# Block products in the first experts' second product and in the fourth attention layer

## The chip, the cores and the metric

One core of one Trainium2 chip runs the whole program. The metric is the device time of one execution in microseconds, the median of three runs. The shares and timelines below come from one profiled execution of the same program.

## The reference, cut to what matters

Two layers of a graph transformer on 1250 nodes with 768 channels, all in float32. Each layer adds graph attention (two attention layers each) and a kernel-feature mixer to its input, then a mixture of experts:

```
x = x + gnn0(ln(x)) + mix0(ln(x))
x = x + ffn0(ln(x))       # 2 of 4 experts, chosen once for all rows
xn = ln(x)
x = x + gnn1(xn) + mix1(xn)
x = x + ffn1(ln(x))

# ffn0, each chosen expert e, its activation gelu, silu, mish or gelu:
h = act_e(x @ w1[e] + b1[e])          # 768 -> 1536
out += gate_e * (h @ w2[e] + b2[e])   # 1536 -> 768

# gnn, each attention layer:
h = x @ W; e = leaky_relu(h@a_src [src] + h@a_dst [dst])
alpha = softmax of e over the edges of each target
out = sum over edges of alpha * h[src] + b
```

## The kernel before

The graph is turned into a dense 1250 x 1250 matrix of edge counts early on, and attention is done densely: for a group of 250 targets the weights ET1 (exp, times the counts) are made for all 1250 sources, and their product with the features HN1 gives the outputs; a column of ones behind the features gives the sum of the weights. Rows come in 10 tiles of T = 125 or in 5 pairs of 250; HALF is 384 channels. Five engines run their own instruction lists and meet in semaphores. TensorE writes into two rings of PSUM banks: five "V" banks that VectorE reads, three "A" banks that ScalarE reads. `plan()` lists the order in which names take banks; `fill` makes TensorE wait until the bank's last user is read (`v_drained` or `a_drained`), and reads are counted in the order of the list.

The experts (PE lines 799 to 805, ScalarE 1229 to 1262, VectorE 1845 to 1955) run 11 iterations u; a unit u is one expert e = u // 5 and one pair of tiles. TensorE makes the first product of unit u in six blocks of 2 x 128 hidden channels (matmuls of 128 x 250, six per 128 channels), then the second product of unit u - 1: four banks, each 12 matmuls of 384 columns. ScalarE drains each block into HB with the bias, then an exp (L1240) one block behind it (three behind in unit 1); `gelu(u)` (L1232) works on the whole unit, for unit 0 behind the third block of unit 1. VectorE computes from the exp the ratio that silu and mish need, in `clamp` (L1848) and `ratio` (L1856 to L1866, seven operations in all on 128 x 500), combines it with the Gelu (L1930), and adds the four banks of unit u - 1, times the gate, to XN (L1948). From u = 6 on it also takes statistics (`pair_output`), from u = 7 on the layer's norm and residual (`pair_residual`, which takes a slot that SP loads) and the next norm (`pair_next`). SP's list issues the DMAs in order: `residual` stores a tile, waits until it is stored and, by its `reused`, until `pair_next` has read it, loads the tile after next and then calls `mixer_load`, which loads the next mixer's weights: WQ lies over the experts' scratch memory, and `q1` (the next mixer's first product) waits for it.

The fourth attention layer's product is `gat1(3)`: five groups of 250 targets, each four banks (two tiles of targets, two halves of channels) of 10 matmuls (one per tile of sources). VectorE makes a group's weights with `larger` (L1720) and a multiply by the counts (L1772) from ScalarE's two rows of exps (`step1`, L1126 and L1131, which for group i start when group i - 2's last bank is full); `drain_group` (L1730 to L1741) divides by the sum of weights, adds to Y, takes statistics, and in tiles 5 and 7 makes the scale of a norm group with `scale`, which waits for ScalarE's square root (`deviation`, L1023); for tile 5 that stands in ScalarE's list behind `step1` of group 4.

The last experts' product and the second mixer's k and v already use block products: for a product of 2 x 2 blocks, seven products of sums of blocks in place of eight, in banks a, b and c that are read and refilled between them.

Of the kernel before, what the change touches and what calls it, by code (L numbers as in the profile page):

```python
# [47 lines left out]
SLOPE = 0.2  # L48
H0, C0 = 4, 192
# [42 lines left out]
def plan():  # L92
# [6 lines left out]
    def gat(layer):  # L99
# [17 lines left out]
        elif layer == 2:  # L117
            for g in range(5):
                V.extend((("acc", 2, g, 0), ("sum", g), ("acc", 2, g, 1), ("acc", 2, g, 2)))
        else:  # L120
            V.extend(("acc", layer, g, i) for g in range(5) for i in range(4))
# [47 lines left out]
    for u in range(11):  # L169
        if u < 10:  # L170
            A.extend(("f1", u, i) for i in range(6))
        if u > 0:
            V.extend(("f2", u - 1, i) for i in range(4))
# [31 lines left out]
def gps_kernel(nc, w, out):  # L205
# [16 lines left out]
    with ctx:  # L222
# [72 lines left out]
        CO = small(16)  # L295
        IS = small(2, 4)
# [70 lines left out]
        TURNED = [mem(C_AT + 6250, 2, 250), mem(C_AT + 6750, 2, 250), mem(F_AT + 11536, 2, 250)]  # L367
        WSUM = [ROW[3][:, i * 250:(i + 1) * 250] for i in range(2)]
# [10 lines left out]
        def hn_pair(layer, t, half):  # L379
            if layer == 0:  # L380
# [11 lines left out]
        EB = mem(C_AT, HM, 250)  # L392
        TB = mem(C_AT + 3000, HM, 250)
        SLOT_F = [mem(C_AT + 6000 + i * D, D) for i in range(2)]
# [72 lines left out]
        prow_loaded = [sem(f"target_rows_loaded{i}") for i in range(2)]  # L467
        slopes_made, larger_made = sem("slopes_made"), sem("larger_made")
# [10 lines left out]
        clamped, expd, t_made, gelu_made, act_made = (sem("hidden_clamped"), sem("hidden_exp"), sem("hidden_exp_used"),  # L479
                                                      sem("gelu_made"), sem("hidden_made"))  # L480
# [23 lines left out]
        def _(pe):  # L504
# [250 lines left out]
            def gat1(layer):  # L755
                gat_front(layer)
                pe.wait_ge(a_drained, A_AT[("h", layer, NT - 1, 1)] + 1)
                for g in range(5):
                    pe.wait_ge(et_made, 80 + (layer - 2) * 5 + g + 1)
                    for tt in range(2):  # L760
                        for p in range(2):
                            b = fill("V", ("acc", layer, g, 2 * tt + p))
                            n = HALF + p
                            for j in range(NT):
                                last = mm(b[0:T, 0:n], ET1[g % 2][0:T, j, tt * T:(tt + 1) * T],
                                          HN1[0:T, j, p * HALF:p * HALF + n], j == 0, j == NT - 1)
                            last.then_inc(v_filled, 1)
# [1876 lines left out]
```

## Time and profile before

| what | us |
|---|---|
| median of 3 runs | 2624.5 (2624.4 to 2626.75) |
| the profiled execution | 2625.9 |
| its span | 2624.1 |
| TensorE busy | 2554.6, 97% |
| VectorE busy | 1586.3, 60% |
| ScalarE busy | 769.3, 29% |

A float32 matmul shows as two records in the trace. The first experts' stage runs from 1010 to 1627 us, the fourth attention layer's product from 2267 to 2396 us.

### The profile page before, as it was taken

The numbers are of one execution on the slowest core, as the hardware profiler recorded it, in microseconds if no ns is written. First come the engines' busy times: TensorE is split into PE (matmuls) and PEld (weight loads), VectorE is DVE, ScalarE is ACT, GpSimd is POOL, SyncE is SP. The second block draws the span as 40 slices with busy tenths as digits, with TensorE's granted clock in tenths as the row PEclk, the third lists the DMA queues.
The fourth block names the chain that finished last, engine by engine and source line by source line (L and its number), as shares of the span: only waits on it lengthen the run. The fifth ranks groups of instructions, "written<-read, shape, count | busy, mean of one in ns | idle before, by whom it ended". The sixth has DMA issues, their size and how long they took to land.

```text
span 2624.1 us, 26650 instructions
## 1 busy us (share of the span) xinstructions
PE 2554.6 (97%) x10594; PEld 1815.0 (69%) x10594; DVE 1586.3 (60%) x2708; ACT 769.3 (29%) x1291; POOL 346.9 (13%) x197
## 2 busy tenths in 40 slices
PE   7999999999999997999999999999999999999999
PEld 4667667658966996777777775565755786556676
DVE  4456471789948996988888998254342561341422
ACT  1143343006733763222222221430002331332000
POOL 0888888000000000000000000000000000000000
PEclk9999999999999998999999999999999999999999
DMA  9232313543020406000120003100450100213201
GB/s 257 26 43 14 50 2 50 140 157 114 20 80 27 110 1 215 1 0 1 72 102 0 24 24 122 64 1 1 119 160 18 37 1 1 64 36 126 87 24 59
DMA packets 139168, 160.74 MB, mean 61 GB/s; under 512 B 96618, under 2 KB 108484, under 8 KB 137516
## 3 DMA queue, kind: packets, MB, share of 16 engines
q1 hardware_dynamic: 68323, 158.60, 19.5%
q0 software_dynamic: 70720, 0.43, 2.8%
q8 instruction: 84, 1.38, 0.2%
q14 instruction: 41, 0.34, 0.0%
HBM read 122.75 MB, written 35.87 MB: 60 GB/s over the span
## 4 chain that ended last, share of the span: by engine, by line
PE 52%; DVE 7%; ACT 2%; issue 1%; DMA 0%; SPq 0%; DVEq 0%; ACTq 0%
PE psum L521 51%; DVE arena L1864 2%; DVE arena L1865 1%; DVE arena L1866 1%; PE psum L532 0%; DVE arena L1857 0%; ACT arena L1126 0%; ACT arena L1131 0%; ACT arena L1015 0%; DVE arena L1519 0%; DVE arena L1930 0%; DVE arena L1361 0%; DVE arena L1863 0%; DVE arena L1856 0%; DVE arena L1889 0%
## 5 line engine op out<-in xcount | busy, mean ns | idle before, releaser
L521 PE MATMUL psum<-arena 128*125 128x384 f32 (+12 forms) x9762 | 2453.4, 413 | 33.9 <-DMA arena<-in_ffn_w 7.2
L521 PEld LDWEIGHTS psum<-arena 128*125 128x125 f32 (+3 forms) x9762 | 1719.4, 188 | 744.1 <-issue 134.7
L2279 POOL DMA_INDIRECT count_matrix<-arena x170 | 342.2, 2013 | 121.5 <-DVE arena L1458 59.6
L1864 DVE RECIPROCAL arena<-arena 128x500 f32<-128x500 f32 x60 | 196.7, 3278 | 2.1
L1613 DVE CUSTOM_DVE_ANT_0 arena<-arena 125x1250 bf16<-125x1250 bf16 (+1 forms) x100 | 139.2, 1458 | 11.7 <-DMA arena<-source_rows 7.1
L2289 POOL MEMSET arena<- 125x60 f32 x1 | 0.2, 211 | 1039.6 <-PE psum L521 1039.6
L1698 DVE TENSOR_TENSOR arena<-arena 125x1250 f32<-125x1250 f32 x80 | 116.3, 1453 | 12.9 <-ACT arena L1108 12.2
L1105 ACT ACTIVATE arena<-arena 125x1250 f32<-125x1250 f32 x80 | 106.9, 1336 | 54.5 <-PE psum L521 54.3
L1701 DVE SCALAR_TENSOR_TENSOR arena<-arena 125x1250 f32<-125x1250 f32 x80 | 116.9, 1461 | 2.8
L1015 ACT ACTIVATE arena<-psum 128x250 f32<-128x250 f32 (+1 forms) x102 | 40.6, 495 | 231.4 <-PE psum L532 230.9
L1248 ACT ACTIVATE arena<-psum,arena 128x250 f32<-128x250 f32 x120 | 49.3, 465 | 199.0 <-PE psum L521 199.0
L1058 ACT ACTIVATE arena<-arena 32x500 f32<-32x500 f32 (+1 forms) x108 | 59.1, 548 | 164.7 <-DVE arena L1492 163.9
L1108 ACT ACTIVATE arena<-arena 125x1250 f32<-125x1250 f32 x80 | 105.8, 1322 | 0.0
L1150 ACT ACTIVATE arena<-psum 125x384 f32<-125x384 f32 x80 | 38.5, 487 | 223.9 <-PE psum L521 123.8
L532 PE MATMUL psum<-arena 125*128 125x125 f32 x420 | 60.0, 290 | 24.0 <-DVE arena L1380 10.8
L1240 ACT ACTIVATE arena<-arena 128x500 f32<-128x500 f32 x60 | 37.3, 621 | 140.0 <-DVE arena L1848 139.9
L1126 ACT ACTIVATE arena<-arena 125x250 f32<-125x250 f32 x100 | 40.4, 490 | 116.4 <-PE psum L521 116.4
L532 PEld LDWEIGHTS psum<-arena 125*128 125x128 f32 x420 | 47.7, 148 | 37.7 <-issue 18.9
L1720 DVE TENSOR_TENSOR arena<-arena 125x2500 f32<-125x2500 f32 x10 | 27.6, 2764 | 72.8 <-ACT arena L1131 72.8
L1631 DVE TENSOR_SCALAR arena<-arena 125x40 f32<-125x40 f32 (+1 forms) x4 | 0.7, 178 | 106.5 <-ACT arena L1150 78.3
L1490 DVE TENSOR_SCALAR arena<-psum,arena 96x500 f32<-96x500 f32 (+1 forms) x36 | 23.3, 647 | 66.0 <-PE psum L521 65.5
L1848 DVE TENSOR_SCALAR arena<-arena 128x500 f32<-128x500 f32 x60 | 25.0, 420 | 61.1 <-ACT arena L1248 59.7
(226 smaller groups left out, 1437.2 us busy)
## 6 DMA issues: line engine op xcount, KB each, us to landing
arena<-in_ffn_w SPq DMA_DIRECT2D x3, 4608.0 KB, 14.8
residual<-arena SPq DMA_DIRECT2D x30, 336.0 KB
arena<-residual SPq DMA_DIRECT2D x30, 336.0 KB
arena<-target_rows SPq DMA_DIRECT2D x12, 610.4 KB
arena<-in_gat_w SPq DMA_DIRECT2D x3, 2304.0 KB, 10.9
arena<-residual SPq DMA_DIRECT2D x10, 672.0 KB
residual<-arena SPq DMA_DIRECT2D x10, 672.0 KB
count_matrix<-arena SPq DMA_DIRECT2D x2, 3125.0 KB, 26.5
```

The costliest lines, as they stand in the source:

```text
L521: return pe.matmul(o, lhsT, rhs, start=start, stop=stop, skip_group_check=share)
L532: last = pe.transpose(b[:, i * T:(i + 1) * T], source[0:T, t0 + i, k * 128:(k + 1) * 128], IDENT[0:T, 0:T])
L1015: act.activation(o, i, ACT.Copy).then_inc(a_drained, 1)
L1058: act.activation(o[low, cols], t[32 * i:32 * i + 32, cols], ACT.Square)
L1105: act.activation(ET4[n % 4][0:T, :], PROWS[layer][h % 2][0][0:T, :], ACT.Exp, bias=ASC[0:T, h, j:j + 1])
L1108: act.activation(E24[n % 2][0:T, :], PROWS[layer][h % 2][1][0:T, :], ACT.Exp, bias=AS2[0:T, h, j:j + 1]).then_inc(slopes_made, 1)
L1248: last = act.activation(HB[u % 2][:, m, :], b[:, j * 250:(j + 1) * 250], ACT.Identity, bias=B1C[:, e, m:m + 1])
L1613: ins = dve.tensor_tensor_reduce(SUMS[n % 2][0:T] if layer < 2 else E24[n % 2][0:T, :], NEG[0:T, t, :], ASROWS[layer][h % 2][0:T, :], 1.0, ...
L1698: dve.tensor_tensor(et, et, E24[n % 2][0:T], ALU.max).then_inc(larger_made, 1)
L1701: dve.scalar_tensor_tensor(et, et, 1.0, CT[0:T, j, :], ALU.min, ALU.mult).then_inc(et_made, 1)
L1864: now(dve.reciprocal(t_, t_))
L2279: pool.indirect_dma_start(counts[k], bass.IndirectOffsetOnAxis(ap=IDX_I[0:T, c:c + 1].bitcast(U32), axis=0), COUNT_I[0:T, c:c + 1], None, ...
```

## The change

In the experts' second product the 12 blocks of 128 hidden channels are split: the first six, as 2 x 2 blocks of three with the two tiles of rows and the two halves of channels, go through seven products of three matmuls; the last six go through four runs of six matmuls, added in the same banks. Five matmuls of 385 columns in each of seven products replace the 40 of a group in the fourth attention layer. `down0`, on TensorE:

```
+            def down0(u):
...
+                bank_d, bank_b, bank_c, bank_a = (fill("V", ("f2", u, i)) for i in "dbca")
+                n = 4 * u
...
+                product(1, bank_a, True).then_inc(parts_filled, 1)
+                pe.wait_ge(hidden_sums, u + 1)
+                pe.wait_ge(w2_sums, u // 5 + 1)
+                product(5, bank_b, True).then_inc(parts_filled, 1)
+                rest(1, 1, bank_d, True)
+                pe.wait_ge(parts_read, n + 1)
+                product(6, bank_a).then_inc(parts_filled, 1)
+                pe.wait_ge(parts_read, n + 2)
+                product(3, bank_b, False, False)
+                rest(0, 1, bank_b)
+                pe.wait_ge(parts_read, n + 3)
+                product(7, bank_a).then_inc(parts_filled, 1)
+                product(2, bank_c, True, False)
+                rest(0, 0, bank_c)
+                pe.wait_ge(parts_read, n + 4)
+                product(4, bank_a, False, False)
+                rest(1, 0, bank_a)
```

On ScalarE the exp reads HB (no clamp before it), with a scale per expert, into one of two small buffers, and a Square follows it; Gelu works in place. On VectorE:

```
+                dve.tensor_scalar(t_, EB[n % 2], BIG, 1.0, ALU.min, ALU.add).then_inc(exp_read, 1)
+                dve.wait_ge(exp_read, n + 1)
+                now(dve.reciprocal(t_, t_))
+                now(dve.tensor_scalar(t_, t_, c(NCK), c(KO), ALU.mult, ALU.add))
+                ins = dve.tensor_tensor(t_, t_, h, ALU.mult)
...
+            def weight2_sums(e):
+                dve.wait_ge(f2_loaded[e], 16)
...
+                now(dve.tensor_tensor(W2T[0], w12, w11, ALU.subtract))
+                now(dve.tensor_tensor(W2T[1], w22, W2T[0], ALU.subtract))
+                step(dve.tensor_tensor(W2T[2], w21, W2T[1], ALU.subtract))
+                now(dve.tensor_tensor(w12, w22, w12, ALU.subtract))
...
+            def sums_of_hidden(u):
...
+                now(dve.tensor_tensor(HS0, a21, a22, ALU.add))
+                step(dve.tensor_tensor(HS1, HS0, a11, ALU.subtract))
+                now(dve.tensor_tensor(a21, a11, a21, ALU.subtract))
+                step(dve.tensor_tensor(HS3[0], a12[:, 0:1], HS1[:, 0:1], ALU.subtract))
+                now(dve.tensor_tensor(HS3[1], a12[:, 1:3], HS1[:, 1:3], ALU.subtract))
```

The sums of W2 are of 1152 columns each, those of the hidden block of 375 (three), 125 and 250.

VectorE's order in an iteration of the experts (`add_part` reads a bank that is filled again, `add_bank` frees one):

```
             for u in range(11):
                 if u < 10:
+                    for i in range(4):
+                        if (u, i) == (6, 3):
+                            weight2_sums(1)
+                        ratio(u, i)
+                if u > 0:
+                    down = {x: bank(("f2", u - 1, x)) for x in "dbca"}
+                    add_part(u - 1, 1, "a", 0, 0)
+                    add_part(u - 1, 2, "b", 1, 1)
+                if u < 10:
+                    ratio(u, 4)
+                if u > 0:
...
+                    add_bank(u - 1, "d", 1, 1)
+                    add_part(u - 1, 3, "a", 0, 1)
+                if u < 10:
+                    ratio(u, 5)
+                if u > 0:
...
+                    add_bank(u - 1, "b", 0, 1)
...
+                    add_part(u - 1, 4, "a", 1, 1)
+                if u < 10:
...
                     dve.wait_ge(gelu_made, u + 1)
+                    dve.scalar_tensor_tensor(HB[u % 2], HB[u % 2], KG[:, e:e + 1], TB, ALU.mult, ALU.add).then_inc(act_made, 1)
...
+                    sums_of_hidden(u)
                 if u == 0:
                     last_bias()
+                    weight2_sums(0)
+                if u == 10:
+                    pair_residual(3)
+                if 7 <= u < 10:
                     pair_residual(u - 7)
                 if u == 10:
                     pair_next(3)
                 if u > 0:
...
+                    add_bank(u - 1, "c", 0, 0)
+                    add_bank(u - 1, "a", 1, 0)
...
+                if u < 5:
+                    add_bias(u)
                 if u >= 6:
                     pair_output(u - 6)
                 if 7 <= u < 10:
                     pair_next(u - 7)
```

The fourth attention layer, TensorE and then VectorE (`spread(g)`, whose banks b, c, a hold 385 columns; RAW keeps three raw sums in SBUF until their weight sum is whole):

```
+                    product(1, bank_a, parts_filled, True)
+                    pe.wait_ge(weight_sums_made, g + 1)
+                    product(5, bank_b, parts_filled, True)
+                    pe.wait_ge(hn_sums, 1)
+                    pe.wait_ge(parts_read, SPREAD_PARTS + 4 * g + 1)
+                    product(6, bank_a, parts_filled)
+                    pe.wait_ge(parts_read, SPREAD_PARTS + 4 * g + 2)
+                    product(3, bank_b, v_filled)
+                    pe.wait_ge(parts_read, SPREAD_PARTS + 4 * g + 3)
+                    pe.wait_ge(hn_sums, 3)
+                    product(7, bank_a, parts_filled)
+                    product(2, bank_c, v_filled, True)
+                    pe.wait_ge(parts_read, SPREAD_PARTS + 4 * g + 4)
+                    product(4, bank_a, v_filled)
...
+                    part(1)
+                    dve.tensor_copy(r00, bank_a[0:T, wide]).then_inc(parts_read, 1)
...
+                    part(2)
+                    dve.tensor_copy(r11, bank_b[0:T, wide]).then_inc(parts_read, 1)
...
+                    part(3)
+                    dve.tensor_copy(r01, bank_a[0:T, wide]).then_inc(parts_read, 1)
+                    if g < 4:
+                        larger(n, g + 1)
...
+                    dve.tensor_tensor(r01, r01, bank_b[0:T, wide], ALU.add).then_inc(v_drained, 1)
+                    if g < 4:
+                        weights(n, g + 1)
+                    part(4)
+                    dve.tensor_tensor(r11, r11, bank_a[0:T, wide], ALU.add).then_inc(parts_read, 1)
+                    if g < 4:
+                        block_sums(n, g + 1)
...
```

Behind that `spread` makes two reciprocals and adds the four halves, times them, to Y, the last two when banks c and a are full; statistics, variance and `scale` follow as before. For group 0 the sums of features (HNT, 1925 columns each) stand between the parts.

SP's list:

```
-                    load(WQ, w["mix1_wq"], m1w[0])
+                    load(WQ[:, 0:5], w["mix1_wq"][:, 0:5], m1w[0])
                 if t == 9:
-                    vf(("f2", 9, 3))
+                    vf(("f2", 9, "b"))
+                    load(WQ[:, 5:6], w["mix1_wq"][:, 5:6], m1w[0])
+                    for k, name in ((1, "mix1_bo"), (2, "mix1_bk"), (3, "mix1_bv")):
+                        row_load(k, name, m1_small)
+                    vf(("f2", 9, "a"))
                     load(WF[1], w["mix1_wk"], m1w[1])
```

The three row loads stood behind the load of the second expert's W2 before. `q1` waits for both parts of WQ.

## Rows read from the trace of the kernel before

**Rows 1.** the page: busy time of each engine and its instructions.
```profile
PE 2554.6 (97%) x10594; PEld 1815.0 (69%) x10594; DVE 1586.3 (60%) x2708; ACT 769.3 (29%) x1291; POOL 346.9 (13%) x197
```

**Rows 2.** waits of TensorE: for whom, us, times, longest.
```profile
PE psum L521 <- DVE arena L1948: 0.6, 1, 0.6
```

**Rows 3.** timeline, VectorE, units 5 and 6: start us, us, line.
```profile
1342.99 3.34 DVE L1930 SCALAR_TENSOR_TENSOR arena<-arena 128x3000 f32<-128x3000 f32 x1
...
1404.30 3.34 DVE L1930 SCALAR_TENSOR_TENSOR arena<-arena 128x3000 f32<-128x3000 f32 x1
```

**Rows 4.** timeline, ScalarE, drains of two blocks of unit 7.
```profile
1426.57 0.83 ACT L1248 ACTIVATE arena<-psum,arena 128x250 f32<-128x250 f32 x2 [2.30 <-PE psum L521]
...
1431.63 0.83 ACT L1248 ACTIVATE arena<-psum,arena 128x250 f32<-128x250 f32 x2 [3.72 <-PE psum L521]
```

**Rows 5.** windows, fourth attention product: us, busy (instructions), granted clock, DMA.
```profile
2266.00:2396.00 130.00, 129.40 (x401) 1.00 0.14 49
```

**Rows 6.** windows, TensorE, while pairs of the second mixer run.
```profile
1716.00:1780.00 64.00, 64.00 (x200) 1.00 0.00 0
```

**Rows 7.** timeline, VectorE, reciprocals of two ratio steps in turn.
```profile
1426.11 3.28 DVE L1864 RECIPROCAL arena<-arena 128x500 f32<-128x500 f32 x1
...
1433.11 3.28 DVE L1864 RECIPROCAL arena<-arena 128x500 f32<-128x500 f32 x1
```

**Rows 8.** groups of VectorE: count, busy us, mean ns, idle before.
```profile
L1864 DVE RECIPROCAL arena<-arena 128x500 f32<-128x500 f32 x60 | 196.7, 3278 | 2.1
...
L1857 DVE TENSOR_TENSOR arena<-arena 128x500 f32<-128x500 f32 x60 | 40.7, 679 | 2.1
...
L1930 DVE SCALAR_TENSOR_TENSOR arena<-arena 128x3000 f32<-128x3000 f32 x10 | 33.4, 3344 | 0.4
...
L1856 DVE TENSOR_SCALAR arena<-arena 128x500 f32<-128x500 f32 x60 | 32.1, 536 | 11.8 <-ACT arena L1240 11.3
...
L1848 DVE TENSOR_SCALAR arena<-arena 128x500 f32<-128x500 f32 x60 | 25.0, 420 | 61.1 <-ACT arena L1248 59.7
...
L1948 DVE SCALAR_TENSOR_TENSOR arena<-psum,arena 125x384 f32<-125x384 f32 x40 | 22.4, 611 | 6.4 <-PE psum L521 6.2
...
L1978 DVE TENSOR_TENSOR arena<-arena 128x375 f32<-128x375 f32 x9 | 4.9, 541 | 0.0
...
L1965 DVE TENSOR_TENSOR arena<-arena 128x1152 f32<-128x1152 f32 x2 | 2.7, 1358 | 0.1
```

**Rows 9.** timeline, ScalarE, unit 1: Gelu of unit 0, sixth block's drain.
```profile
1060.79 2.70 ACT L1232 ACTIVATE arena<-arena 128x3000 f32<-128x3000 f32 x1
...
1073.83 0.83 ACT L1248 ACTIVATE arena<-psum,arena 128x250 f32<-128x250 f32 x2 [0.52 <-PE psum L521]
```

**Rows 10.** timeline, units 9, 10: residual, bank adds, SP's DMAs, transposes.
```profile
1593.78 0.17 DVE L1881 RECIPROCAL arena<-arena 125x2 f32<-125x2 f32 x1
...
1603.00 2.19 DVE L1948 SCALAR_TENSOR_TENSOR arena<-psum,arena 125x384 f32<-125x384 f32 x4
...
1609.47 0.79 SPq L2305 DMA_DIRECT2D residual<-arena  x2
...
1613.19 0.75 SPq L2305 DMA_DIRECT2D arena<-residual  x2
...
1626.99 2.94 PE L532 MATMUL psum<-arena 125*128 125x125 f32 x24
```

**Rows 11.** timeline, attention product, start of group 3.
```profile
2344.48 4.05 ACT L1126 ACTIVATE arena<-arena 125x250 f32<-125x250 f32 x10 [17.86 <-PE psum L521]
...
2353.78 0.21 ACT L1023 ACTIVATE arena<-arena 125x4 f32<-125x4 f32 x1
```

**Rows 12.** windows, timeline: TensorE after stops of 2.85, 1.45, 5.27 us.
```profile
144.00:148.00 4.00, 2.64 (x6) 0.61 0.68 121
...
612.00:616.00 4.00, 4.00 (x26) 1.00 1.03 411
...
990.17 5.03 PE L532 MATMUL psum<-arena 125*128 125x125 f32 x24 [5.27 <-ACT arena L1034]
```

More of the change, by code:

```diff
@@ L757, in gat1 @@
                 pe.wait_ge(a_drained, A_AT[("h", layer, NT - 1, 1)] + 1)
-                for g in range(5):
[L759 to L767, printed above, removed]
+                low, high = slice(0, 5), slice(5, 10)
@@ L1231, in gelu @@
                 act.wait_ge(t_made, u + 1)
-                act.activation(EB, HB[u % 2], ACT.Gelu).then_inc(gelu_made, 1)
+                act.activation(HB[u % 2], HB[u % 2], ACT.Gelu).then_inc(gelu_made, 1)
             for u in range(10):
@@ L1236, in _ @@
                 act.wait_ge(b1_loaded, 32)
+                act.wait_ge(choice_made, 1)
                 def expo(i):
-                    act.wait_ge(clamped, 6 * u + i + 1)
-                    act.activation(EB[:, 2 * i:2 * i + 2, :], TB[:, 2 * i:2 * i + 2, :], ACT.Exp).then_inc(expd, 1)
+                    n = 6 * u + i
+                    if n >= 2:
+                        act.wait_ge(exp_read, n - 1)
+                    act.wait_ge(a_drained, A_AT[("f1", u, i)] + 1)
+                    x = EB[n % 2]
+                    act.activation(x, HB[u % 2][:, 2 * i:2 * i + 2, :], ACT.Exp, scale=SCL[:, e:e + 1]).then_inc(act_step, 1)
+                    own[0] += 1
+                    act.wait_ge(act_step, own[0])
+                    act.activation(x, x, ACT.Square, bias=MISH[:, e:e + 1]).then_inc(expd, 1)
                 lag = 3 if u == 1 else 1
@@ new lines, in block_sums @@
+                def block_sums(n, g):
+                    dve.wait_ge(et_made, n + 1)
+                    et = ET1[g % 2][0:T]
+                    a11, a12, a21, a22 = (et[:, 5 * j:5 * j + 5, i * T:(i + 1) * T] for i in range(2) for j in range(2))
+                    now(dve.tensor_tensor(ES0[0:T], a21, a22, ALU.add))
+                    step(dve.tensor_tensor(ES1[0:T], ES0[0:T], a11, ALU.subtract))
+                    now(dve.tensor_tensor(a21, a11, a21, ALU.subtract))
+                    dve.tensor_tensor(ES3[0:T], a12, ES1[0:T], ALU.subtract).then_inc(weight_sums_made, 1)
@@ L1761, in drain_turned @@
                             dve.engine_nop().then_inc(v_drained, 1)
-                drain = drain_turned if layer == 2 else drain_group
-                if layer == 2:
-                    dve.wait_ge(ct_loaded, 32)
+                if layer == 3:
+                    dve.wait_ge(a_drained, A_AT[("h", 3, 4, 1)] + 1)
+                    first = step(dve.tensor_tensor(HNT[0][0:T], hn[0][1], hn[0][0], ALU.subtract))
+                    larger(85, 0)
+                    weights(85, 0)
+                    dve.wait_ge(a_drained, A_AT[("h", 3, 9, 1)] + 1)
+                    after(first)
+                    block_sums(85, 0)
+                    feature_sum(1, hn[1][1], HNT[0][0:T])
+                    for g in range(5):
+                        spread(g)
+                    return
+                drain = drain_turned
+                dve.wait_ge(ct_loaded, 32)
                 for g in range(6):
@@ L1832, in _ @@
             after(own[0])
+            step(dve.tensor_scalar(SCL, MISH, 0.5, 0.5, ALU.mult, ALU.add))
             now(dve.scalar_tensor_tensor(NCK, CC, -1.0, KO, ALU.mult, ALU.mult))
+            dve.engine_nop().then_inc(choice_made, 1)
             dve.wait_ge(gate_exp, 1)
```

196 lines of the change are left out of this document (129 added, 67 removed).

## The prediction

> **What bounds the kernel now.** I read the busy table first, then who TensorE waited for, then the timeline around both edited stages. TensorE is busy 97% of the span while VectorE is at 60% [rows 1]: the time is the matmuls' own time plus TensorE's stops, and a matmul less is worth its duration unless a stop takes its place. In the first-experts stage (from 1010 to 1627 us) TensorE stops once for VectorE, 0.6 us on the bank adds of L1948 [rows 2]. VectorE is near its limit there without costing anything: the finished hidden block is used only after the next unit's first product, some 30 us later. So the question is how much of this slack the change spends.
>
> **Matmuls saved.** A unit repeats every 61.31 us (1342.99 to 1404.30 in [rows 3]). Its first product fills a bank every 5.06 us, six of them 30.4 us [rows 4]; the 48 matmuls of the second take the other 30.9, 0.645 each. `down0` issues 7x3 + 4x6 = 45, so 10 units save 30 x 0.645 = 19.4 us. The fourth attention product takes 129.4 us for 200 matmuls (two records each), 0.647 each [rows 5]; 35 instead of 40 in each of 5 groups save 25 x 0.647 = 16.2 us. Together 35.6 us if nothing new waits.
>
> Many small runs of matmuls over changing banks cost nothing extra by themselves: the second mixer's pairs already work so, and their stretch has no idle time and a granted clock of 1.00, the 2.4 GHz level [rows 6]. The Trainium skill (TensorE: Matmul & The Clock Gate, "A second HAM failure mode: psum-queue depth-cycling") says the contrary, that going round the PSUM banks in each iteration lets the clock swing between its levels; by that rule this change would lose far more than it saves. Rows 6 disagree for just this pattern, so it keeps only the small chance below.
>
> **VectorE's new work.** A ratio step has seven operations today, 7.00 us from one to the next [rows 7, 8]. The new one has four: min/add 0.42, reciprocal 3.28, scale 0.54, multiply 0.68, with gaps 5.0 us, less than the 5.06 in which a block arrives. Priced by their nearest rows in [rows 8]: sums of the hidden block 2.4 us (0.54 for 375 columns, five of them, two smaller), W2 sums 4 x 1.36 + gaps = 5.6, bias add 1.9 (two of 768 columns, between the 0.54 of 375 and the 1.36 of 1152), each bank add 0.6, activation combine 3.34. Eight bank adds instead of four are 2.4 us. ScalarE's extra Square is 0.62; it waits for banks most of the time, so it is hidden, and would cost at most 6 x 0.62 a unit if it weren't. In all VectorE gets about 5 us of work less in an ordinary unit. What counts is order: the banks are read in the middle of a unit, and TensorE waits for four of the reads.
>
> **Ordinary unit**, counted from its start: ratio 3 (counting from 0) starts at 27.4 (block 4 full at 25.3, drain 0.8, exp and square 1.2) and ends at 32.4. Products 1 and 5 end at 32.3 and 34.2; the two adds are done by 34.9, and product 6 wants the first at 38.1. Ratio 4 ends at 39.9, the next two adds at 41.1, and product 7 wants them at 45.9; ratio 5 ends at 46.1, the last two at 48.5, and product 4 wants that at 53.6. About 5 us to spare at each, so nothing is lost. Four places are not ordinary.
>
> **Unit 1.** The Gelu of unit 0 still stands behind the third block of unit 1: 1060.79 + 2.70 = 1063.5 [rows 9], and VectorE, now quicker, only waits for it. Then come combine (1066.9), hidden sums (1069.3), last_bias 1.7 (1071.0), W2 sums (1076.6), the bias add that moved forward (1078.5), four ratios (1098.3), the first bank add (1098.9). TensorE ends its first product at 1073.8 [rows 9], runs product 1, waits 1.0 for the W2 sums, runs 5 and the six matmuls of bank d, and is at 1082.5 before product 6: it waits 16.4. Before, the same VectorE queue delayed nobody. Bounds: -2 to +3, because all terms are rows.
>
> **Unit 6.** The second expert's W2 sums (5.6) stand before ratio 3 and delay product 5 from 32.3 to 33.8: 1.5 us, between 0 and 3.
>
> **Unit 9.** It has no first product ahead. `down0` asks for all four banks at its head, and bank a needs unit 8's bank c read, which VectorE does only after `pair_residual(2)`. From unit 9's start: ratio 5's use of h ends at 46.1, Gelu 48.8, combine 52.2, sums 54.6, residual 9.2 (1593.78 to 1603.00, [rows 10]) 63.8, add 64.4; TensorE is there at 30.4 + 29.0 = 59.4. It waits 5.0, against 0.6 now: +4.4, between 0 and 7.
>
> **q1.** WQ's last sixth is loaded behind tile 9's residual load in the SP queue, and that behind the store of tile 7 and `pair_next(3)`. VectorE now starts `pair_residual(3)` only after the fourth part of unit 9. From the end of `down0(8)`: fourth part read 25.2 (5.0 + 2.2 for the clock, 27 matmuls 17.4, add 0.6), residual 34.4, normalise 36.3, store to next load 3.7 (1609.47 to 1613.19, [rows 10]) and the issues 41.8, landing some 3.5 more, 45.3. TensorE is ready at 5.0 + 2.2 + 29.0 + 3.7 (transposes, [rows 10]) = 39.9. Wait 5.3, between 0 (its own slack) and 9.
>
> **Attention, group 3.** Block sums (4 x 0.81 for 625 columns, between 0.68 for 500 and 1.36 for 1152 in [rows 8]) just fit beside product 1's 3.2: 0.1 us. In the tail of group 2 VectorE waits in `scale(2, 0)` for ScalarE's deviation, which stands behind the twenty exps of step 4: 2344.48 to 2353.99 [rows 11], and two short operations make the scale by 2354.4. Today that is harmless. Now group 3's first part can't be read before +10.5 us, and product 6 wants it at +6.5: 4.0 us, between 3 and 5. Groups 1, 2 and 4 have 2 us or more to spare.
>
> **The clock.** A stop longer than a couple of us is followed by a stretch at 1.2 GHz: after 2.85 us idle the granted clock was 0.61 in the next 4 us, after 5.27 idle 24 transposes took 5.03 us where 24 others took 2.94 [rows 10], so 2.1 to 2.2 lost; after 1.45 us idle it stayed 1.00 [rows 12]. For four such stops 3 x 2.2 + 1.7 = 8.3 us, between 0 and 11.
>
> **Sum.** -35.6 + 1.0 + 16.4 + 1.5 + 4.4 + 5.3 + 0.1 + 4.0 + 8.3 = +5.4 us. The profiled execution, 2625.9 (span 2624.1), should become 2631.3 (span 2629.5); it lies 1.4 above the median of the three runs, 2624.5, so I forecast 2629.9, rounded 2630.0. What a measurement can tell from no change is about 0.2%, 5.2 us.
>
> **Rivals.**
> - *The hold in unit 1 is missing, faster.* Were product 6 of unit 1 served in time, 16.4 + 2.2 go: 2611; with unit 9 and q1 served too, 2594. For it: VectorE's total work falls, and in ordinary units it keeps up. Against: the queue of unit 1 is a plain sum of rows. It decides if the first add comes before 1082.5 instead of 1098.9. Chance 0.14.
> - *The stops are there, but the clock falls less*, or the slack in q1's chain covers its load: 5 to 9 us less, 2621 to 2625, same. For it: the penalty differs from stop to stop in rows 12. Chance 0.17.
> - *VectorE becomes the bound from unit 7 on*, where residual, statistics and next input are in its loop (5 us later per unit than reckoned eats the spare of 5), or BQ1, now queued behind the row loads and WK, makes q1's banks wait: 5 to 10 us more, 2635 to 2640, slower. Against: today's units 7 to 9 carry more VectorE work with one stop of 0.6. Chance 0.13.
> - *The bank rule quoted above.* If only a tenth of the 625 changed matmuls (450 and 175) ran at 1.2 GHz, 62 x 0.65 = +40 us, 2670. Chance 0.01.
>
> **Chances.** The forecast itself (2625 to 2635) has 0.55, with more than half of it beyond the 0.2% line at 2629.7. So faster 0.15, within 0.2% 0.38, slower 0.47. Range 2615 to 2638: it takes the clock rival and most of the slower one, and the nearer edge of the fast one.
>
> **What would show it.** In the profile after: an idle stop of about 16 us before matmuls near 1082 released by L1948's successor; stops of about 5 near unit 9's start (by VectorE) and before q1 (by the DMA of in_mix_wq); one of 4 early in the attention product's fourth group (group 3); the clock below 1.00 behind each; none in units 2 to 5, 7 and 8, which then repeat in about 59.4 us; attention groups of 22.7 us but one of about 29. The forecast is wrong if the stop in unit 1 is under 10 us, or if stops add up to more than 45.

## The result, and the profile after

The changed kernel takes 2634.4 us (median of 7 runs, 2630.7 to 2635.9), the one before 2625.4 (7 runs, 2624.4 to 2626.8): ratio 1.0033, 95% interval 1.0022 to 1.0044. It is slower, by 9 us or a third of a per cent. The forecast was 2630.0, with 2615 to 2638 as its range. The profiled execution took 2632.8 us (span 2630.8).

The page of the profile after, its busy row (answers to [rows 1]):

```profile
PE 2529.6 (96%) x10484; PEld 1796.7 (68%) x10484; DVE 1560.9 (59%) x2681; ACT 815.2 (31%) x1351; POOL 347.5 (13%) x197
```

TensorE is busy 25.0 us less, and the span is 6.7 us longer. Not all 35.6 us of dropped matmuls show in the busy time: some of those that stayed took twice as long (9.3 us in all, worked out below). Idle time grew by the other 31.7 us. The waits of TensorE, after (for whom, us in all, times, longest; in [rows 2] the experts' stage had one such wait, of 0.6 us):

```profile
PE psum L535 <- DVE arena L2044: 20.9, 2, 16.1
...
PE psum L535 <- DMA arena<-in_mix_wq: 5.8, 1, 5.8
...
PE psum L535 <- DVE arena L1842: 4.2, 1, 4.2
...
PE psum L535 <- DVEq L2026: 2.8, 2, 2.0
```

L2044 is the bank add, L1948 before; L1842 the first copy of a bank in the attention layer's `spread`; L2026 the signal that the sums of W2 are made. The timeline of TensorE, after (start us, us, and in brackets the idle time before, with what ended it):

```profile
1076.11 6.04 PE L535 MATMUL psum<-arena 128*125 128x384 f32 x18 [0.85 <-DVEq L2026]
1098.21 294.10 PE L535 MATMUL psum<-arena 128*125 128x384 f32 x1152 [16.06 <-DVE arena L2044]
1394.29 205.48 PE L535 MATMUL psum<-arena 128*125 128x384 f32 x786 [1.97 <-DVEq L2026]
1604.58 31.40 PE L535 MATMUL psum<-arena 128*125 128x384 f32 x90 [4.81 <-DVE arena L2044]
1635.82 2.94 PE L546 MATMUL psum<-arena 125*128 125x125 f32 x24
1644.56 33.05 PE L535 MATMUL psum<-arena 128*128 128x500 f32 x72 [5.81 <-DMA arena<-in_mix_wq]
...
2283.14 74.73 PE L535 MATMUL psum<-arena 125*125 125x385 f32 x230 [1.45 <-ACT arena L1230]
2362.03 40.77 PE L535 MATMUL psum<-arena 125*125 125x385 f32 x120 [4.15 <-DVE arena L1842]
```

These are the stops of the forecast, in their places. Between the one at 1098 and the one at 1394 lie four whole iterations (u = 2 to 5) in one unbroken row. The combine of the hidden block, which repeated in 61.31 us in [rows 3], now repeats in 59.38:

```profile
1230.43 3.34 DVE L2132 SCALAR_TENSOR_TENSOR arena<-arena 128x3000 f32<-128x3000 f32 x1
...
1289.81 3.34 DVE L2132 SCALAR_TENSOR_TENSOR arena<-arena 128x3000 f32<-128x3000 f32 x1
```

How the 16.06 us come about is to be read on VectorE. ("Unit 1" is iteration u = 1, in which `down0(0)`, the second product of unit 0, runs.) Its timeline, after, from the first Gelu to the end of the hold:

```profile
1063.14 3.34 DVE L2132 SCALAR_TENSOR_TENSOR arena<-arena 128x3000 f32<-128x3000 f32 x1 [7.97 <-ACT arena L1312]
...
1070.50 1.36 DVE L2022 TENSOR_TENSOR arena<-arena 128x1152 f32<-128x1152 f32 x1
...
1077.81 0.42 DVE L2007 TENSOR_SCALAR arena<-arena 128x500 f32<-128x500 f32 x1
...
1097.55 1.14 DVE L2044 SCALAR_TENSOR_TENSOR arena<-psum,arena 125x384 f32<-125x384 f32 x2
```

VectorE first idles 7.97 us for ScalarE's Gelu (L1312), then has the combine, the hidden sums, the bias rows, the W2 sums and a bias add ahead of it (14.7 us, to 1077.81), then four ratios (19.7 us), and only then the add for which TensorE has stood since 1082.15.

The windows of TensorE behind the two longest of the new stops, as in [rows 12] (us, busy and instructions, granted clock, DMA share, GB/s; a clock of 0.50 is the 1.2 GHz level, 1.00 the 2.4 GHz level):

```profile
1100.00:1102.00 2.00, 2.00 (x4) 0.50 0.00 0
1102.00:1104.00 2.00, 2.00 (x5) 0.57 0.00 0
1104.00:1106.00 2.00, 2.00 (x8) 1.00 0.00 0
...
1644.00:1646.00 2.00, 1.44 (x2) 0.50 0.86 164
1646.00:1648.00 2.00, 2.00 (x3) 0.50 1.04 253
1648.00:1650.00 2.00, 2.00 (x4) 0.53 1.10 432
```

A matmul that begins at 1098.21 and a window 1102 to 1104 at 0.57 (1.72 us of it at half speed) make 5.5 us at 1.2 GHz, half of which is lost: 2.75. In the same way: 4.3 us behind the stop at 1604 (2.15 lost), 5.3 behind the one at 1644 (2.65), 3.4 behind the one at 2362 (1.7). Behind the 1.97 us at 1394 the clock stayed at 1.00.

**Where the time went**, from the first matmul of the experts (1010.39 before, 1009.79 after) to the end of q1's first part (1660.95 and 1677.45): 650.6 us became 667.7, +17.1. The attention product took 129.3 (2266.60 to 2395.91) and takes 119.5, -9.8. Ahead of the experts 0.6 us went, in code that is the same in both kernels, and all the rest is equal to 0.1 us: +6.7 in the profiled pair.

### The profile page after: what moved, and what is told of

The parts are those of the page before. It is cut to its first block, busy times and chain, and to the rows that moved or that the text cites. A ratio compares the mean times of both kernels' runs of the same rounds, so it can differ in the third digit from the quotient of the medians.

```text
span 2630.8 us, 26552 instructions
## 1 busy us (share of the span) xinstructions
PE 2529.6 (96%) x10484; PEld 1796.7 (68%) x10484; DVE 1560.9 (59%) x2681; ACT 815.2 (31%) x1351; POOL 347.5 (13%) x197
## 3 DMA queue, kind: packets, MB, share of 16 engines
q8 instruction: 83, 1.36, 0.2%
## 4 chain that ended last, share of the span: by engine, by line
PE 54%; DVE 4%; ACT 2%; DMA 1%; issue 1%; SPq 0%; DVEq 0%; ACTq 0%
PE psum L535 53%; DVE arena L2009 1%; ACT arena L1206 1%; ACT arena L1211 1%; PE psum L546 0%; DVE arena L1607 0%; ACT arena L1095 0%; PE psum L663 0%; DVE arena L2132 0%; DMA out<-arena 0%; DVE arena L2011 0%; ACT arena L1312 0%; DVE arena L2074 0%; DVE arena L2010 0%; DVE arena L1449 0%
## 5 line engine op out<-in xcount | busy, mean ns | idle before, releaser
L535 PE MATMUL psum<-arena 128*125 128x384 f32 (+13 forms) x9652 | 2429.2, 413 | 66.5 <-DVE arena L2044 20.9
L535 PEld LDWEIGHTS psum<-arena 128*125 128x125 f32 (+4 forms) x9652 | 1702.0, 188 | 769.8 <-issue 161.6
L2044 DVE SCALAR_TENSOR_TENSOR arena<-psum,arena 125x384 f32<-125x384 f32 x80 | 47.7, 613 | 48.1 <-PE psum L535 47.2
L1312 ACT ACTIVATE arena<-arena 128x3000 f32<-128x3000 f32 x10 | 27.0, 2703 | 101.9 <-DVE arena L2011 101.9
```

What stands on the lines that cost most here:

```text
L535: return pe.matmul(o, lhsT, rhs, start=start, stop=stop, skip_group_check=share)
```

## The experiments

Twelve kernels, each beside runs of the kernel before on its chip (2625.6 to 2626.0 us in the three sets). The whole program's time moves by 2 us or so between executions, at times by 5, in part by when the first expert's weights land: the experts' first matmul came anywhere from 1008.6 to 1013.8 us in these profiles. The changed kernel was not run again beside them: "less" below is against its median of 2634.4 from its own seven runs, and is good to 2 us or so. So I give a second number: in the profiled execution, the stage from that matmul to the end of q1's first part ("stage": 650.6 before, 667.7 changed), which does not depend on when it starts. It is one execution each, and not free of chance either: the wait for WQ in front of q1 was 5.81 us in the changed kernel, but 6.78 in `scale_later`, which changes nothing near it.

**The two halves of the change.** `attention_only` keeps the old experts, `experts_only` the old attention layer.

> Only the fourth attention layer's product has the seven block products; the first experts are as before. Theory: the product keeps its 25 matmuls less (16.2 us), and gives back the stop of group 3 (4.15 us in the profile of the changed kernel) and the stretch at 1.2 GHz behind it (about 1.7 us), so some 9.8 us less than before: 2615 to 2617. Rival 1, the two edits lean on each other (the attention stop comes from something that the experts' part leaves behind): the stop is not there, 2608 to 2611. Rival 2, the attention part's own cost is larger than its trace in the joint kernel shows: 2620 or more.

Measured 2616.3 (5 runs, ratio 0.9960, 0.9946 to 0.9973). Stage 650.7, attention product 120.1.

> Only the first experts' second product and the edits that make room for it; the attention layer is as before. Theory: 19.4 us of matmuls go, 16.1 + 0.9 + 2.0 + 4.8 + 5.8 us of stops come, and three stretches at 1.2 GHz behind the long ones of some 2.2 to 2.8 us each: about 17 to 19 us more than before, 2642 to 2645. Rival: part of the joint kernel's loss is its attention part meeting changed weights, rows or banks, and this one is below 2638.

Measured 2643.1 (5 runs, 1.0065, 1.0051 to 1.0079). Stage 667.3. Minus 9.3 and plus 17.5 make 8.2 together, against the 9 of the joint change: within what these medians can tell, the halves don't lean on each other. The attention half is a gain by itself, and the experts' half loses it and as much again. The attention stop in `attention_only`:

```profile
2345.11 41.40 PE L528 MATMUL psum<-arena 125*125 125x385 f32 x120 [4.15 <-DVE arena L1784]
```

**Is the slow clock behind a stop a cost of its own?** `hold_busy` fills the stop of unit 1 with matmuls whose result is overwritten.

```diff
                 rest(1, 1, bank_d, True)
+                if u == 0:
+                    for e in range(24):
+                        mm(bank_c[0:T, 0:HALF], left[0][e % 3], right[0][:, e % 3, :], e == 0, e == 23, share=True)
                 pe.wait_ge(parts_read, n + 1)
```

> The changed kernel with 24 matmuls of 125x384 more (a product of the first block, into the third bank, which the next product with a start overwrites) in the place in unit 1 where TensorE waits 16.06 us for the first partial sum to be read. They take 24 x 0.645 = 15.5 us if the clock stays at 2.4 GHz. Theory: the wait's end is set by VectorE and does not move; the stop shrinks to about 0.6 us, and the matmuls behind it run at 2.4 GHz at once instead of some 5.5 us at half of it, so 2.7 us less than the changed kernel: 2631 to 2632. Rival 1, the slow stretch has another cause than the idle engine (the order of banks, the load behind it): no change, 2634, and the granted clock behind the place still 0.50. Rival 2, the product that waits is not set by VectorE's reading: the added matmuls add their 15.5 us, 2650.

Measured 2631.0 (11 runs, 1.0017, 1.0008 to 1.0026), 3.4 under the changed kernel though it does 24 matmuls more. Stage 665.2, 2.5 less, with a wait for WQ of 7.0. The stop is 0.58 us, the clock is 1.00 behind it, and the row from there to unit 6 is 2.71 us shorter (291.39 against 294.10). Timeline and a window of `hold_busy`:

```profile
1099.26 291.39 PE L535 MATMUL psum<-arena 128*125 128x384 f32 x1152 [0.58 <-DVE arena L2047]
```

```profile
1099.00:1103.00 4.00, 3.74 (x12) 1.00 0.02 4
```

`hold_half` adds 12 instead of 24.

> hold_busy with 12 matmuls more instead of 24: 7.7 us of the stop of 16.06 us are filled, 8.3 us stay. It asks whether the slow stretch behind a stop shrinks with the stop. Theory 1 (a stop of several us costs about the same stretch whatever its length, as the 4.8, 5.8 and 16.1 us stops of the changed kernel left 4.3, 5.3 and 5.5 us of it): 2.0 to 2.8 us of loss stay, 2634 to 2635. Theory 2 (the loss goes with the length of the stop): about 1.4 us of loss, 2633. The times can hardly tell these apart; the granted clock in the profile behind the stop does.

Measured 2635.9 (5 runs, 1.0036, 1.0022 to 1.0050), stage 667.6. The time is a little above both forecasts and decides nothing; the clock does. The stop is 8.32 us, and the slow stretch is as long as behind 16.06: from 1100.41 to 1105.9, 5.5 us. The timeline's row, and its windows:

```profile
1100.41 294.08 PE L535 MATMUL psum<-arena 128*125 128x384 f32 x1152 [8.32 <-DVE arena L2047]
```

```profile
1104.00:1105.00 1.00, 1.00 (x2) 0.50 0.00 0
1105.00:1106.00 1.00, 1.00 (x3) 0.56 0.00 0
1106.00:1107.00 1.00, 1.00 (x4) 1.00 0.00 0
```

So halving the stop gives nothing back of the clock, and filling it gives all.

**What holds TensorE in unit 1?** `unit1_reads` changes two orders on VectorE.

```diff
+                early = 2 if u == 1 else 0
...
-                    for i in range(4):
+                    for i in range(4 - early):
...
-                    ratio(u, 4)
+                    ratio(u, 4 - early)
...
-                    ratio(u, 5)
+                    for i in range(5 - early, 6 - early // 2):
+                        ratio(u, i)
...
+                if u == 1:
+                    ratio(1, 5)
+                if u == 0:
+                    last_bias()
+                    weight2_sums(0)
+                    add_bias(0)
                 if u < 10:
                     e = u // 5
                     dve.wait_ge(gelu_made, u + 1)
...
```

(The same three calls go from their old places further down.)

> The changed kernel with two orders on VectorE altered. The bias rows, the four sums of W2 and the bias sum of chunk 0 stand before the wait for the first Gelu (where VectorE is idle 7.97 us) instead of behind it, and in unit 1 alone the partial sums are read after the second, third, fourth and fifth ratio instead of after the fourth, fifth, sixth and sixth. Theory: product 6 has its bank read before TensorE gets there, the stop of 16.06 us, the one of 0.85 us and the stretch at 1.2 GHz (2.7 us) all go: 19 to 20 us less than the changed kernel, 2614 to 2616. Rival 1, the hold only moves to a later product of the same unit (product 7 or 4), since VectorE's six ratios take 30 us whatever their order: 2620 to 2628. Rival 2, the hold was hiding ScalarE's or VectorE's lateness in unit 2, which now stops TensorE by about as much: 2630 or more.

Measured 2618.0 (6 runs, 0.9970, 0.9958 to 0.9982): 16.4 us less, not 19 to 20. Stage 650.9, 16.8 less. The cause is the right one and the rest is to be seen in its timeline:

```profile
1099.49 275.91 PE L535 MATMUL psum<-arena 128*125 128x384 f32 x1104 [1.29 <-DVE arena L2044]
1377.38 207.18 PE L535 MATMUL psum<-arena 128*125 128x384 f32 x786 [1.98 <-DVEq L2026]
```

1.29 us are left, because I had put the fourth read behind five ratios; and the stop of unit 6, as long as ever, was this time followed by a slow stretch (207.18 us where the others have 205.48). Its halves, `sums_only` (the bias and W2 sums sooner) and `reads_only` (unit 1's reads sooner, the fourth now behind four ratios):

> One half of unit1_reads alone: the bias rows, the four sums of W2 and the bias sum of chunk 0 stand before VectorE's wait for the first Gelu; the partial sums are read in the changed kernel's order. Theory (the hold is VectorE's queue in front of the first read, which moves with everything that is taken out of it): VectorE's first ratio of unit 1 starts some 7.9 us sooner than at 1077.81, so the stop shrinks from 16.06 to about 9 us (TensorE comes to it 0.85 us sooner, since the sums it waited for are made), the slow stretch behind it stays: 8 us less than the changed kernel, 2626 to 2627. Rival (the hold is set by ScalarE's exponentials of unit 1, which follow their own order): 2632 or more.

> The other half: in unit 1 the partial sums are read after the second, third, fourth and fourth ratio, the sums of W2 stay behind the first Gelu. Theory: the first read comes two ratios (2 x 4.93 us) sooner, so the stop shrinks from 16.06 to about 6.2 us and the slow stretch stays: 10 us less than the changed kernel, 2624 to 2625. The two halves together then make the whole (8 + 10 us against the 16.9 us of both stops that are there to take). Rival: the read in front of ratios makes the later ones wait for TensorE, and product 7 or 4 stops as well: 2628 or more.

Measured 2624.6 (11 runs, 0.9995, 0.9986 to 1.0005) and 2623.8 (11 runs, 0.9996, 0.9987 to 1.0006), stages 657.7 and 657.5 (2626 to 2627 and 2624 to 2625 were expected). The stops, from the timelines of `sums_only` and then of `reads_only`:

```profile
1090.39 292.95 PE L535 MATMUL psum<-arena 128*125 128x384 f32 x1152 [9.21 <-DVE arena L2044]
```

```profile
1088.05 293.93 PE L535 MATMUL psum<-arena 128*125 128x384 f32 x1152 [6.19 <-DVE arena L2044]
```

16.06 us less 9.87 is 6.19, two ratios to the hundredth. The hold is VectorE's queue in front of the first read: whatever is taken out of that queue comes off the stop. The stage of `sums_only` shrank by 10.0 us where its stops account for 7.7; the rest is mostly shorter slow stretches (1.15 us behind the hold, 292.95 against 294.10, and 0.6 in unit 9). The halves' 10.0 and 10.1 us add up to more than the 16.8 of `unit1_reads`, for three reasons: their stops together would be 0.7 us more than the 16.9 that are there, and `unit1_reads` alone has the stop of 1.29 and the 1.7 us behind unit 6.

The other way to shorten the queue is an earlier Gelu. `gelu_sooner`:

```diff
-                    if (u, i) == (1, 2):
+                    if (u, i) == (1, 1):
                         gelu(0)
```

> The changed kernel with ScalarE's first Gelu behind the second drain of unit 1 instead of behind the third. Theory: it can start at 1055.2 (when VectorE has made its last ratio) instead of 1060.3 with its table, so all of VectorE's work behind it, with the read that ends the hold, comes 5.1 us sooner: stop of about 11.8 us instead of 16.06 + 0.85, 5 us less than the changed kernel, 2629 to 2630. Rival (the drains that now stand behind the Gelu hold TensorE's banks in unit 1): TensorE gets new stops in 1050 to 1065 and the time stays above 2632.

Measured 2626.6 (11 runs, 1.0004, 0.9995 to 1.0013), 7.8 less where 5 were expected. The stop is 12.09 us (11.8 expected), the 0.85 is gone, and the stage is 6.5 us shorter: 4.8 of stops and about 1.5 of shorter slow stretches. The 1.3 between stage and median lie in the executions' spread (2623.3 to 2632.1). No new stops in unit 1.

**The other three stops.** `scale_later` moves one short step of VectorE that waits for ScalarE. In the changed kernel's timeline this step (L1463) stands right in front of the first copy (L1842):

```profile
2361.04 0.18 DVE L1463 RECIPROCAL arena<-arena 125x4 f32<-125x4 f32 x1 [6.48 <-ACT arena L1103]
...
2361.33 0.55 DVE L1842 COPY arena<-psum 125x385 f32<-125x385 f32 x1
```

The edit:

```diff
                     dve.tensor_copy(r01, bank_a[0:T, wide]).then_inc(parts_read, 1)
+                    if g == 3:
+                        scale(2, 0)
...
-                        if t in (5, 7):
-                            scale(2, t // 6)
+                        if t == 7:
+                            scale(2, 1)
```

> The changed kernel with VectorE's first step for the normalisation of tiles 0 to 3 (a reciprocal that waits for a square root which ScalarE does only after the exponentials of group 4) moved from the end of group 2's draining to behind the third copy of group 3. Theory: the first two copies of group 3 stand ready at 2354.6, before TensorE needs them, so the stop of 4.15 us and the slow stretch behind it (1.7 us there, 2.4 in the attention part alone) go: about 6 us less than the changed kernel, 2628 to 2629. Rival 1, the wait was also ScalarE's lateness with the weights of group 4: TensorE stops there instead and the gain is under 2 us, 2632 or more. Rival 2, ScalarE's normalisation comes later now and delays the transposes or the products behind the layer: 2634 or more.

Measured 2628.2 (11 runs, 1.0009, 1.0000 to 1.0018), 6.2 less; attention product 113.4, 6.1 less. The product runs through, and nothing behind it is late (timeline of `scale_later`):

```profile
2285.34 113.58 PE L535 MATMUL psum<-arena 125*125 125x385 f32 x350 [1.45 <-ACT arena L1230]
2398.75 5.95 PE L546 MATMUL psum<-arena 125*128 125x125 f32 x48
```

`wq_sooner` issues the load of WQ's last slice before SP turns to the residual of tiles 6 to 9:

```diff
                     load(WQ[:, 0:5], w["mix1_wq"][:, 0:5], m1w[0])
-                if t == 9:
                     vf(("f2", 9, "b"))
                     load(WQ[:, 5:6], w["mix1_wq"][:, 5:6], m1w[0])
+                if t == 9:
```

> The changed kernel with the load of WQ's last slice (384 KB) issued right behind the load of its first five (at 1613.95 in the profile), once unit 9's bank b is read (1623.2), instead of at 1640.80, behind four more stores and loads of the residual on SP. Theory: the slice is there before TensorE ends its transposes at 1638.8, the stop of 5.81 us shrinks to the 0.7 us of the bank's turn, and the slow stretch behind it (2.7 us) goes: 7 to 8 us less than the changed kernel, 2626 to 2628. Rival 1, the drains of q1 wait for BQ1, which lands at 1656.7 whatever is done here; with TensorE 5 us ahead its banks run full before that and the stop comes back there: 2631 to 2634. Rival 2, the residual's transfers on SP come late by the wait and VectorE's last pairs with them: 2634 or more.

Measured 2628.6 (11 runs, 1.0006, 0.9997 to 1.0015), 5.7 less, stage 4.4 less. It falls between theory and first rival, and the timeline shows why:

```profile
1641.31 15.36 PE L535 MATMUL psum<-arena 128*128 128x500 f32 x36 [0.73 <-ACT arena L1095]
1659.47 15.36 PE L535 MATMUL psum<-arena 128*128 128x500 f32 x36 [2.81 <-ACT arena L1374]
```

WQ is there in time, but half way through the product the banks are full: ScalarE's first drain waits for BQ1 (3 KB), queued behind the 2304 KB load of WK. The changed kernel has that wait too, where the stop of 5.81 covered it (its timeline of ScalarE):

```profile
1656.75 0.21 ACT L1356 ACTIVATE arena<-arena 128x6 f32<-128x6 f32 x1 [16.70 <-DMA arena<-in_mix_bq]
```

`unit9_reads`: unit 8's bank c is added before `pair_residual`, and unit 9's first two parts before the statistics (`pair_output` gets the count of drains taken before them).

```diff
-                if u > 0:
+                if 0 < u < 10:
                     down = {x: bank(("f2", u - 1, x)) for x in "dbca"}
...
-                if 7 <= u < 10:
-                    pair_residual(u - 7)
...
                     add_bank(u - 1, "c", 0, 0)
+                if 7 <= u < 10:
+                    pair_residual(u - 7)
...
+                n = count[0]
+                if u == 9:
+                    down = {x: bank(("f2", 9, x)) for x in "dbca"}
+                    add_part(9, 1, "a", 0, 0)
+                    add_part(9, 2, "b", 1, 1)
                 if u >= 6:
-                    pair_output(u - 6)
+                    pair_output(u - 6, n)
```

> The changed kernel with unit 8's bank c added before the residual of pairs 0 to 2 instead of behind it, and, in the last unit, the first two partial sums of unit 9 read before the statistics and the normalisation of the next pairs instead of behind them. Theory: TensorE finds bank c free when it comes to unit 9, and its first two sums read when it needs them, so the stop of 4.81 us and the 2.2 us at 1.2 GHz go: 6 to 7 us less than the changed kernel, 2627 to 2629. What can give it back: the WQ slice, which is tied to SP's residual transfers and these to VectorE's pairs, not to TensorE. Rival 1, those transfers do not move, so TensorE reaches q1 earlier by 7 us and waits there by about 7 us more, in all nothing: 2633 to 2635. I hold these two about equally likely. Rival 2, VectorE's pairs end later and q1's second part waits: 2636 or more.

Measured 2625.6 (11 runs, 1.0001, 0.9992 to 1.0010), 8.8 less where 6 to 7 were expected, but the stage is 6.0 less; the difference is the spread of the medians. Unit 9 begins with no stop, and the load of WQ comes forward with it but for 1 us (timeline of `unit9_reads`):

```profile
1393.64 234.51 PE L535 MATMUL psum<-arena 128*125 128x384 f32 x876 [1.97 <-DVEq L2026]
1627.98 2.94 PE L546 MATMUL psum<-arena 125*128 125x125 f32 x24
1637.77 32.78 PE L535 MATMUL psum<-arena 128*128 128x500 f32 x72 [6.85 <-DMA arena<-in_mix_wq]
```

The rival (the load is tied to the residual's transfers, so the wait grows by as much, some 7 us) is not borne out: those transfers follow TensorE, too. Nor does the wait of 6.85 against 5.81 show a small part of it, since `scale_later` has 6.78 and `hold_busy` 7.02 without this edit.

**All together.** `all_mended` has the edits of `unit1_reads` (with `reads_only`'s fourth read), `scale_later`, `wq_sooner` and `unit9_reads`, not the sooner Gelu, and besides W2's sums of the second expert in front of ratio 2 instead of ratio 3, and BQ1 loaded ahead of WK.

> The changed kernel with all five edits: unit 1's reads sooner and its sums before the first Gelu (now with the fourth read behind the fourth ratio, which takes the 1.29 us that were left), unit 6's sums of W2 one ratio sooner, unit 9's reads, the WQ slice behind the first five, BQ1 ahead of the two large loads, and the scale of tiles 0 to 3 later. Theory, by the sum of the stops and of the slow stretches in the changed kernel's profile: 16.1 + 0.9 + 2.0 + 4.8 + 5.8 + 4.2 = 33.8 us of stops and 2.8 + 2.2 + 2.7 + 1.7 = 9.4 us of clock, 43 us less than the changed kernel: 2591 to 2595, which is the time before less the 36 us of matmuls that the block products save, with what is left over. Rival 1, the stops have stood in for each other (one only shows because another is gone): a new one of 5 to 10 us, at the end of q1 or in units 7 to 9, where VectorE is busiest, and 2598 to 2606. Rival 2, VectorE's order takes over as the bound in the units 7 to 9: 2610 or more.

Measured 2591.0 (4 runs, 2590.3 to 2593.6; ratio to before 0.9871, 0.9856 to 0.9886): faster than both kernels, 34.9 us under the one before beside it (2626.0). Its TensorE timeline through the experts and q1:

```profile
1008.64 367.91 PE L535 MATMUL psum<-arena 128*128 128x250 f32 x1482 [7.10 <-DMA arena<-in_ffn_w]
1378.16 228.73 PE L535 MATMUL psum<-arena 128*125 128x384 f32 x858 [1.61 <-DVE arena L2046]
1606.73 2.94 PE L546 MATMUL psum<-arena 125*128 125x125 f32 x24
1610.40 30.45 PE L535 MATMUL psum<-arena 128*128 128x500 f32 x72 [0.73 <-ACT arena L1095]
```

The stage takes 632.0 us and the attention product 113.4. Against before that is -18.5 and -15.9, together 34.4 of the 35.6 us that the missing matmuls are worth. What is left is the stop of 1.61 in unit 6: the W2 sums are there in time now, and their 5.4 us on VectorE delay the first read instead. Earlier is not enough there; those sums would have to leave a unit whose reads have 5 us to spare.

## Why the prediction was right

| Step (forecast) | Forecast us | Measured us |
|---|---|---|
| matmuls | -35.6 | not directly; 34.4 realised in `all_mended` |
| product 5 of unit 1 | +1.0 | +0.85 |
| product 6 of unit 1 | +16.4 | +16.06 |
| unit 6 | +1.5 | +1.97 |
| unit 9 | +4.4 | 4.81 - 0.62 = +4.2 |
| q1 | +5.3 | 5.81 - 0.73 = +5.1 |
| attention, block sums and group 3 | +4.1 | +4.15 |
| clock behind stops | +8.3 | +9.3 |
| sum | +5.4 | +6.0 by the terms, +6.7 by the spans |

Each stop was priced within 0.5 us, from durations in the rows of before. The reasoning that carried it: count not how much work VectorE has but what stands in front of each read that TensorE waits for, with every wait in that queue. `reads_only` and `sums_only` show this for the largest, `scale_later`, `wq_sooner` and `unit9_reads` for the other three, and `all_mended` for their sum.

**What was off.** *The clock*, mis-sized by 1.0 us: I took 2.1 to 2.2 us a stop, and after shows 1.7 to 2.75. The price rests on the transposes behind 5.27 us alone. The window behind 2.85 us in [rows 12] begins 1.36 us before that stop ends, so it shows no more than 1.3 us lost. The 1.7 that I took for the attention stop had no row, and that it came out as 1.7 is luck: by durations, the slow stretch behind the same stop cost 1.9 us here and up to 3.1 in other profiles. "Longer than a couple of us" was too sure as well: below are stops of under 2 us that had such a stretch behind them and one of 2.81 that had none.

*q1's 5.3* is 5.4 by its own terms (45.3 less 39.9), and its 3.7 for the transposes already holds the turn of the bank (2.94 + 0.73), so it stands against 5.1. In other profiles that stop was up to 1.2 us longer. *The fast rival's 2594* should be 2597 by its own terms. *The ordinary units* were right: 59.38 us against 59.4, no stops in units 2 to 5, 7 and 8. The holds of unit 9 and q1 are separate: mending the first left the second.

*The 0.7 us between terms and spans* is the sum of three differences. The experts' stage lost 0.8 us more than its terms. The attention product lost 0.5 more: 113.4 us without a stop is 15.9 under before and not 16.2, and its slow stretch cost 1.9 by durations. Ahead of the experts 0.6 us went. For the 0.8 I can name no cause.

**From 2630.0 to 2634.4.** 1.3 us is the sum. The other 3 is where the profiled execution lies among its kernel's: before, it was 1.4 above the median on which I set the forecast; after, it lies 1.6 below its own. That part is chance between executions, and no mechanism of the change.

**The rivals.** *The hold in unit 1 is missing* fell with the 16.06 us. *The clock falls less* was wrong: 9.3 us against 8.3. (It stayed at 2.4 GHz behind the 1.97 us of unit 6, but that stop was not among the four priced.) *VectorE becomes the bound from unit 7 on* didn't come, but its second half, BQ1 behind the row loads and WK, was real: it lay hidden under the WQ stop and showed with 2.81 us in `wq_sooner`.

*The bank rule*: from 1104 to 1392 the second products go round four banks, 45 matmuls each in eight runs of three to nine, without a gap, and the row behind the second stop (1394.29, 205.48 us) has this duration to the hundredth in nine of ten kernels in which it runs from the stop of unit 6 to the one of unit 9; from 1106 to 1392 TensorE was busy for all 286 us at a granted clock of 1.00, the 2.4 GHz level. The clock fell only behind idle time. The Trainium skill (TensorE: Matmul & The Clock Gate, "A second HAM failure mode: psum-queue depth-cycling") reports the swinging clock from a kernel of bf16 matmuls with 512 columns, in which TensorE idles for moments between groups. It is not borne out for the pattern here, float32 matmuls of 384 columns in unbroken rows.

## What to carry to other kernels

A transformation that trades matmuls for sums is priced on the engine that makes the sums, read by read: for each wait of TensorE, add up what stands in front of its release on the other engine, waits included, in the first and last turn of a loop as well as in an ordinary one. All the loss here sat in five places, most of them at the edge of a loop, and moving a few operations in their queues (no operation less) turned +9 us into -35. A stop that has gone uncovers the next, smaller one behind it, so mend them together and look again.

## What the hardware showed

- The price of a stop of TensorE is not its length alone. Stops of 4.15 to 16.06 us were followed by 3.2 to 5.8 us at 1.2 GHz, with no relation to their length that I can see (3.2 us behind 9.21 in `sums_only`, 5.5 behind 8.32 in `hold_half`, 5.5 behind 16.06, 5.8 behind 4.15 in `wq_sooner`). Matmuls for nothing in a stop that can't be avoided gave 2.7 us back.
- Around 2 us it goes either way. The stop of 1.97 us in unit 6 cost nothing behind it in ten profiles and 1.7 us in `unit1_reads`; 2.81 us in `wq_sooner` left the clock at 2.4 GHz.
- The plainest case lies ahead of the experts, in code that no kernel here changes. A stop of 1.89 us (1.88 in two) stands at about 915 us in all 14 profiles. In seven of them, before among them, a stretch at 1.2 GHz follows; in the other seven, after among them, the clock stays at 1.00. So the length of a stop does not decide it, and I did not find what does. There the stretch cost nothing in the end: the row behind the stop grew from 33.64 us (after) to 34.63 (before), and the next stop, which VectorE sets as well, shrank from 1.88 to 0.91. The row and a window of before:

```profile
915.71 34.63 PE L521 MATMUL psum<-arena 125*125 125x193 f32 x200 [1.89 <-DVE arena L1671]
```

```profile
916.00:920.00 4.00, 4.00 (x16) 0.57 0.00 0
```

- The same stop of 4.15 us in the attention product cost from 1.9 to 3.1 us more than itself (40.77 us behind it after the change, 41.96 in `wq_sooner`, and 113.58 - 74.73 = 38.85 for the same matmuls without the stop).
